# Moving the PSUM evacuations of the layernorm and the v projection from VectorE to ScalarE

## The reference

```python
x = x + attn(layernorm(x))      # x: (8, 2048, 1024), one batch element per core
x = x + ffn(layernorm(x))

def attn(x):                    # W_qkv: (16, 1024, 192), W_out: (16, 64, 1024)
    qkv = einsum('bsd,ndh->bnsh', x, W_qkv); q, k, v = split(qkv, 3)
    a = softmax(einsum('bnqh,bnkh->bnqk', q, k) / 8 + causal_mask)
    out = einsum('bnqk,bnkh->bnqh', a, v).reshape(B, -1, S)
    return einsum('bds,nhd->bsd', out, W_out)
def ffn(x):                     # w1: (1024, 4096), w2: (4096, 1024)
    return einsum('bsw,wd->bsd', relu(einsum('bsd,dw->bsw', x, w1) + b1), w2) + b2
```

## Time and profile before

| | us |
|---|---|
| median of 2 runs | 1385.1 |
| the two runs | 1368.73, 1401.48 |
| the profiled execution | 1383.07 |
| its span on the slowest core (core 2) | 1381.5 |
| spans of the eight cores | 1353.6 to 1381.5 |
| granted TensorE clock, mean of each core | 0.877 to 0.887 |

### The profile page before, as it was taken

One profiled execution on the slowest core, in us unless ns is written; L12 is line 12 of the kernel. 1 busy time (PEld: TensorE's weight loads), 2 busy tenths in 40 slices (PEclk: granted clock), 3 DMA queues, 4 the chain that ended last, 5 costly groups with the idle time before them and its releaser, 6 DMA issues.

```text
span 1381.5 us, 12666 instructions; the slowest of 8 cores (1353.6 to 1381.5 us)
## 1 busy us (share of the span) xinstructions
PE 1001.5 (72%) x4656; PEld 395.7 (29%) x4656; DVE 530.4 (38%) x686; ACT 364.9 (26%) x395; POOL 100.9 (7%) x131
## 2 busy tenths in 40 slices
PE   1155678958585858585867368898879878988897
PEld 0022332212121212131211033343324333443343
DVE  0454444363635354535443543404331323223201
ACT  0000005647475747575667300000000000000000
POOL 2100020000000000000000001020012011111110
PEclk9988998879797979797987679998989889989899
DMA  9900044100000000200020037897869779896976
GB/s 244 123 0 0 1 38 39 16 0 9 7 9 8 0 1 1 31 1 1 0 31 1 0 43 110 122 151 145 121 101 152 152 101 142 125 181 94 139 116 139
DMA packets 94331, 93.17 MB, mean 67 GB/s; under 512 B 40000, under 2 KB 72768, under 8 KB 94272
## 3 DMA queue, kind: packets, MB, share of 16 engines
q0 software_dynamic: 85248, 75.57, 39.7%
q1 hardware_dynamic: 9024, 16.80, 4.0%
HBM read 159.54 MB, written 8.39 MB: 122 GB/s over the span
## 4 chain that ended last, share of the span: by engine, by line
PE 61%; DVE 17%; DMA 13%; issue 4%; ACT 2%; DVEq 2%; POOL 0%; ACTq 0%; POOLq 0%
PE arena L718 16%; PE arena L673 12%; PE arena L506 10%; DMA wstage<-w 9%; PE arena L363 9%; PE arena L451 5%; PE arena L286 5%; DVE tmp_sb L601 4%; DVE oscr_sb L523 3%; DVE x_sb L612 3%; DMA wstage<-wout 2%; DVEq L51 2%; PE arena L466 2%; PE arena L239 1%; DVE lnf_sb L247 1%
## 5 line engine op out<-in xcount | busy, mean ns | idle before, releaser
L479 ACT ACTIVATE p_sb<-arena,cst_sb 128x1024 bf16<-128x1024 f32 (+1 forms) x320 | 291.2, 986 | 100.0 <-PE arena L451 61.7
L506 PE MATMUL arena<-p_sb,vaug_h 128*128 128x512 bf16 (+3 forms) x640 | 192.6, 387 | 146.6 <-DVE oscr_sb L523 95.3
L673 PE MATMUL arena<-lnf_sb,wstage 128*128 128x512 bf16 x1024 | 252.0, 411 | 63.4 <-DMA wstage<-w 55.8
L718 PE MATMUL arena<-w2stage,h_sb 128*128 128x512 bf16 x1024 | 221.7, 379 | 4.0 <-DVE h_sb L686 4.0
L686 DVE TENSOR_SCALAR h_sb<-arena,b1c_sb 128x512 bf16<-128x512 f32 x128 | 96.1, 751 | 217.4 <-PE arena L673 217.4
L673 PEld LDWEIGHTS arena<-lnf_sb,wstage 128*128 128x128 bf16 x1024 | 105.2, 104 | 209.2 <-issue 109.8
L718 PEld LDWEIGHTS arena<-w2stage,h_sb 128*128 128x128 bf16 x1024 | 99.9, 98 | 125.8 <-issue 5.9
L363 PE MATMUL arena<-lnf_sb,wstage 128*128 128x512 bf16 x512 | 125.1, 401 | 5.2 <-DMA wstage<-wqkv 5.2
L451 PE MATMUL arena<-qpair,kpair 64*128 64x512 bf16 (+3 forms) x640 | 124.8, 386 | 4.8 <-DVE kpair L386 4.8
L203 ACT ACTIVATE rsd_sb<-bag_sb,cst_sb 128x4 f32<-128x4 f32 x8 | 2.4, 298 | 456.3 <-DVE bag_sb L199 456.2
L239 PE MATMUL arena<-identb_sb,lntm_sb 128*128 128x128 bf16 x256 | 27.7, 279 | 109.9 <-DVE lntm_sb L223 97.9
(11 more groups left out here) (37 smaller groups left out, 452.8 us busy)
## 6 DMA issues: line engine op xcount, KB each, us to landing
wstage<-w POOLq DMA_DIRECT2D x32, 1024.0 KB, 10.7
w2stage<-w POOLq DMA_DIRECT2D x64, 512.0 KB, 7.0
x_sb<-x SPq DMA_DIRECT2D x4, 2048.0 KB, 24.9
y<-y_sb SPq DMA_DIRECT2D x16, 512.0 KB, 6.5
wstage<-wqkv POOLq DMA_DIRECT2D x24, 256.0 KB, 12.7
wstage<-wout POOLq DMA_DIRECT2D x4, 512.0 KB, 21.8
b1c_sb<-b SPq DMA_DIRECT2D x32, 0.5 KB, 7.2
identb_sb<-identf POOLq DMA_DIRECT2D x1, 32.0 KB, 8.6
```

The lines of the kernel that those rows point to most:

```text
L479: e.activation(AP(p_sb, (si_ % 3) * 1024, [[3 * 1024, 128], [512, 2], [1, w_]]), AP(arena, b_ + off_, [[AR, 128], [512, 2], [1, w_]]), AF. ...
L506: e.matmul(AP(arena, (4 + hx) * 512 + off_, [[AR, 128], [1, w_]]), vaug_h[:, hx, j_ * 128:(j_ + 1) * 128], AP(p_sb, (si_ % 3) * 1024 + hx ...
L673: (lambda s_, dc_, fb_, wp_: lambda e: e.matmul(bankap(fb_, TF), AP(wstage, s_ * 1024 + dc_ * 512 + wp_ * 128, [[8 * 1024, 128], [1, 128]] ...
L718: (lambda s_, ww_, c2_, dh_, t_: lambda e: e.matmul(bankap(t_, 512), h1_sb[:, ww_, 128 * c2_:128 * (c2_ + 1)], w2stage[:, s_, 512 * dh_:51 ...
```

## The change

The copy in `ln_transpose` and the copy in `emit_v_chunk` are issued on ACT, as an ACTIVATE with the function Identity, in place of a `tensor_copy` on DVE, and raise `ex` instead of `vv`. What waited for them waits for `ex`. The score regions at banks 2, 3 and 6, 7 and the accumulator banks of attention get waits on the last of these copies. Nothing else is changed: tiles, buffers, order of the list and all other operations are as before.

```diff
--- before.py
+++ after.py
@@ -185,7 +185,7 @@
         ln_bank_free = [("vv", 0), ("vv", 0)]
         ln_tm_free = [("tp", 0)] * 4
         ex_rstd_last = [0]
-        lnf_state = {"ready": 0}
+        lnf_state = {"ready": ("ex", 0)}
 
         def ln_stats(src_col, idx, extra_v=()):
             pb = idx % 2
@@ -244,15 +244,16 @@
                     skip_group_check=True))(pb, dc, buf),
                     waits=w0, inc="tp" if dc == DC - 1 else None)
             free_tbl[pb] = ("tp", tp_last)
-            vv_ev = add("vector", (lambda t0, p_, d_: lambda e: e.tensor_copy(
+            ex_ev = add("scalar", (lambda t0, p_, d_: lambda e: e.activation(
                 d_[:, :, t0:t0 + 128],
                 AP(arena, (2 * (p_ % 2)) * 512,
-                   [[AR, 128], [128, 8], [1, 128]])))(
+                   [[AR, 128], [128, 8], [1, 128]]),
+                AF.Identity))(
                 dst_tok0, pb, dst_sb),
-                waits=[("tp", tp_last)], inc="vv")
-            ln_bank_free[pb % 2] = ("vv", vv_ev)
-            lnf_state["ready"] = vv_ev
-            return vv_ev
+                waits=[("tp", tp_last)], inc="ex")
+            ln_bank_free[pb % 2] = ("ex", ex_ev)
+            lnf_state["ready"] = ("ex", ex_ev)
+            return ("ex", ex_ev)
 
         def ln_apply(src_col, idx, dst_sb, dst_tok0, parity, vv_rstd,
                      extra_tp=()):
@@ -267,10 +268,10 @@
                 [[64, NH], [1, HD]])
             wv_slots.append((s, dw))
         v_bank_free = [("vv", 0), ("vv", vv_wb)]
-        vv_vaug_done = 0
+        vv_vaug_done = ("ex", 0)
         last_v_mm = 0
 
-        def emit_v_chunk(c, vv_lnf_c):
+        def emit_v_chunk(c, lnf_c_rdy):
             nonlocal vv_vaug_done, last_v_mm
             pb = c % 2
             b0 = 4 + 2 * pb
@@ -280,7 +281,7 @@
                     s, dwv = wv_slots[dcc]
                     w0 = [dwv]
                     if h == 0 and dcc == 0:
-                        w0 += [("vv", vv_lnf_c), ("vv", vv_vones),
+                        w0 += [lnf_c_rdy, ("vv", vv_vones),
                                v_bank_free[pb]]
                     mm_last = add("tensor",
                                   (lambda s_, h_, dc_, c_, b_: lambda e: e.matmul(
@@ -292,12 +293,13 @@
                                   waits=w0,
                                   inc="mm" if (h == 1 and dcc == DC - 1) else None)
             last_v_mm = mm_last
-            vv_ev = add("vector", (lambda c_, b_: lambda e: e.tensor_copy(
+            ex_ev = add("scalar", (lambda c_, b_: lambda e: e.activation(
                 v_all[:, c_, 0:1024],
-                AP(arena, b_ * 512, [[AR, 128], [1, 1024]])))(c, b0),
-                waits=[("mm", mm_last)], inc="vv")
-            v_bank_free[pb] = ("vv", vv_ev)
-            vv_vaug_done = vv_ev
+                AP(arena, b_ * 512, [[AR, 128], [1, 1024]]),
+                AF.Identity))(c, b0),
+                waits=[("mm", mm_last)], inc="ex")
+            v_bank_free[pb] = ("ex", ex_ev)
+            vv_vaug_done = ("ex", ex_ev)
 
         vv_rstd_q = [0] * 4
         lnf_rdy_t = [None] * TC
@@ -323,9 +325,9 @@
             slot_free[s] = ("mm", last_v_mm)
 
         qk_bank_free = [("vv", 0), ("vv", 0)]
-        s_reg_free = [("ex", 0)] * 3
+        s_reg_free = [vv_lnf1, vv_vaug_done, ("ex", 0)]
         REG_BASE = [1024, 3072, 0]
-        o_bank_free = [("vv", vv_vaug_done), ("vv", vv_vaug_done)]
+        o_bank_free = [vv_vaug_done, vv_vaug_done]
         vv_attn_done = 0
         ex_attn_done = 0
         vaug_free = [("mm", 0), ("mm", 0)]
@@ -355,7 +357,7 @@
                         qb2 = g % 2
                         mm_last = None
                         for dcc in range(DC):
-                            w0 = ([dwqk, ("vv", vv_lnf1),
+                            w0 = ([dwqk, vv_lnf1,
                                    qk_bank_free[qb2]] + list(extra)
                                   if dcc == 0 else [])
                             mm_last = add("tensor",
@@ -408,7 +410,7 @@
                                                [128, TC], [1, 64]]),
                     AP(v_all, 64 * n_, [[TC * 1024, 128],
                                         [1024, TC], [1, 64]])))(n, hix),
-                    waits=[("vv", vv_vaug_done), ("vv", vv_vones),
+                    waits=[vv_vaug_done, ("vv", vv_vones),
                            vaug_free[hix]],
                     inc="vv")
             if npair + 1 < NH // 2:
@@ -667,7 +669,7 @@
                 fb = ww % 4
                 mm_f1 = None
                 for dcc in range(DC):
-                    w0 = ([dww, ("vv", vv_ln2), f1_bank_free[fb]]
+                    w0 = ([dww, vv_ln2, f1_bank_free[fb]]
                           if dcc == 0 else [])
                     mm_f1 = add("tensor",
                                 (lambda s_, dc_, fb_, wp_: lambda e: e.matmul(
```

## The result

The changed kernel takes 1319.5 us (median of 11 runs, 1316.1 to 1323.4) against 1384.7 us for the kernel before on the same chip: a ratio of 0.956 with a 95% interval of 0.953 to 0.959.

The account below looks back on a forecast made before the run. The bound was taken to be v-stage transposes waiting for DVE's apply, queued behind a v cast that waits for PE. From 1383.1 us, 51.9 (stage) and 6.1 (FFN starts) were subtracted: 1325 us, range 1306 to 1349.

Parts of the forecast that it names:

- Price of one copy: PSUM copy on ACT: 1.11 us, taken from the same-shape Exp row; hidden in steady chunks up to 2.0 us.
- Steady chunk: First (v) stage: PE runs back to back, so the period falls from 6.44 to 4.06 us per chunk.
- Start: Start of v stage: v(0) starts at 68.2 and ends at 73.5 us; transposes 3 and v(1) end at 77.5.
- Holes: v stage, chunks 4 and 8: PE waits 2.9 us each behind Sqrt, plus 1.4 us of lost clock each.
- Stage: First transpose to last v matmul: ends at 141.8 instead of 193.7, 51.9 us less; bounds 139.0 to 147.8.
- Attention at nothing: Attention: same instructions per engine, new waits on work already over, so priced at 0.
- FFN starts: Ahead of four FFN groups: lnf copies begin sooner on ACT, 1.6 us in group 0, 1.5 x 3 after, together 6.1.
- more idle time on w1 loads: FFN: a listed sign of being wrong, PE waiting longer for w1 weight loads; no size given.
- A: v stage stays at lower clock: chunk 6.82, stage 118, whole 1366 us, chance 0.04; beside it, 13/16 clock gives about 1340.
- B: ACT reloads tables between Sqrt and Identity, 7 x 1.28 = 9 us on the path: 1334 us; chance 0.08.
- C: Start of attention set by a DMA that doesn't move, up to 52 us lost: 1377 us, no change; chance 0.03.
- D: ACT's copies become the bound, from 2.0 us each; some 5.0 us a copy gives 1413 us; chance 0.01.

Follow-up runs that it names:

- the second profile: The changed kernel run once more with nothing altered, for a second profile: profiled execution 1315.6 us, median 1317.3 us.
- both kernels with half loads: Changed kernel, and the same with lnf copies ahead of FFN back on DVE, each with w1 loads halved in groups 1 to 3: 1288.1 and 1287.9 us.
- the first run of the reordered kernel: Kernel before with apply of chunk c+1 ahead of the v cast of c-2 on DVE, nothing on ACT: executions 1351.9 to 1435.2 us, no ratio.

## Why the prediction was right, and where its terms were off

The bound that it named, an apply behind a v cast that waits for PE, is shown: v alone on ACT and a new order on DVE give the same stage, 88.4 and 88.7 us, and lnf alone leaves it at 123.5.

- *Price of one copy*: 1.11 taken, 1.02 measured. Hidden in the steady chunks, as said: 16 more copies cost 3.7 us, nearly all of it at the two holes.
- *Steady chunk*: 4.06 predicted, 3.90 measured. The 4.06 was read from the first transpose to the end of the last v matmul, and counted the tail of that matmul, over which the next one starts. From start to start it would have been right; 48 matmuls in 10.52 already said 3.5 for a v group instead of 3.62. Over 13 chunks this is 2.1 us.
- *Start*: v(0) at 3.4 us after the first transpose, measured 3.1; v(0) itself 4.7 instead of 5.3; ahead of it PE was idle for 0.4 us, before for 2.4 us twice.
- *Holes*: 2.9 predicted, 2.82 measured, at chunks 4 and 8 and not at 12. Their price in clock, 1.4 taken between 0 and 4.4, is 1.7 and 1.5 (5.30 and 5.09 against 3.62). Taking both holes away saved 8.6 us of 2 x (2.82 + 1.6) = 8.8. The nearest hole was a fair guess and partly luck: the length alone doesn't set the price. With lnf alone on ACT a hole of 2.49 us (ahead of 97.33) was followed by transposes of 0.61 and v matmuls of 3.62, and the next, of 2.50 (ahead of 103.89), by transposes of 1.01.
- *Stage*: 77.0 predicted, 73.9 measured (74.7 on core 2); with its bounds of 74.2 to 83 the mean lies just outside, because the bounds were put on the holes alone and the error was in the steady chunk.
- *Attention at nothing*: right within its scatter; the q/k wait moved with the v matmuls.
- *FFN starts*: 6.1 us predicted as gained and kept. The starts gave more, 8.0. But "the other loads are released by FFN1 matmuls and move with them" failed: w1 waits took back about 5 of the 8. This is the step of the prediction that was wrong, and it is small only because the term was. It looked at the two loads issued ahead, which indeed had landed, and took the later ones to be fixed in length. The prediction had listed "more idle time on w1 loads" as a sign of being wrong, and that sign came.
- *Rivals*: A (the lower level throughout): out, the mean granted clock of the stage rose to 0.95. B: three table loads in all, as before, and none between a Sqrt and an Identity. C: out, the q/k matmuls moved with the last v matmul. D: out, a copy takes 1.02. A granted clock between the two levels, 0.81, came on two cores of the first profiled execution (last section). That this execution took 1339.9 us, near the 1340 named beside A, is chance: its slowest core took 12 us longer in the v stage and 15 in the attention, which the estimate did not contain.

The forecast of 1325 was thus 5.5 us high. By the means of the cores the change is 60.4 us and the sum was 58.0: the stage gave 3.2 more, attention 2.4 more than nothing, the FFN part 2.8 less (3.3 against 6.1). That the errors of stage and FFN cancel is luck. The other 3 us lie in what the sum was subtracted from, the slowest core of one execution (1383.1). That core lay 14 us behind the mean of cores at its last matmul, and the slowest of the changed kernel's profile 7, which no term of the sum could see. If the change brings the cores closer together was not tested.

## What to carry to other kernels

When two engines are each half idle and wait for each other, look at what stands in the in-order queue ahead of the instruction that the bound engine needs; moving an evacuation to an idle engine and moving it behind that instruction in its own queue cure the same steady wait, and the second needs no other engine. Count a period from start to start. And price an earlier start only after asking which stream behind it is at its limit: here a stage fed by DMA took back about 5 of 8 us, while the gain in the v stage, which was bound by engines, was kept.

## What the hardware showed beside this

In the first profiled execution of the changed kernel, cores 2 and 3 ran the steady v chunks at a granted clock that is neither of the two levels. Windows of core 1, then of core 2, for the same 11 us:

```profile
86.00:97.00 11.00, 8.83 (x53) 4.31 (x51) 1.19 (x4) 5.08 (x6) 0.00 (x0) 1.00 0.00 0
...
86.00:97.00 11.00, 11.00 (x61) 5.36 (x59) 2.68 (x6) 5.39 (x6) 0.00 (x0) 0.81 0.00 0
```

And on core 2:

```profile
90.49 0.70 PE L239 MATMUL arena<-identb_sb,lntm_sb 128*128 128x128 bf16 x8
91.01 4.37 PE L287 MATMUL arena<-wstage,lnf_sb 128*128 128x512 bf16 x16
```

Granted 0.81: a v group takes 4.37 where it takes 3.62, transposes 0.70 instead of 0.61, and the stage 85.8 and 85.5 us instead of 74, on two of the four cores of a die. The prediction had weighed the Trainium skill (TensorE: Matmul & The Clock Gate, Part 1, the peak-current limiter), which gives 13/16 = 0.81 for a die with three cores in dense matmuls, and held the trace of before against it. This execution agrees with that figure, 4.37 / 3.62 being 1.21 and 16/13 being 1.23. It does not agree on when: in the second profile all eight cores ran the same dense stage at 73.3 to 74.7 us, and cores 0 and 1 of the same die were not held here. Four more of the fourteen profiles have such stretches, from one moment on (within 1 us) always on both cores of a pair: 2 and 3 in both kernels with half loads, 4 and 5 with lnf alone on ACT, 0 and 1 together with 6 and 7 in the first run of the reordered kernel. Where they begin in the v stage or in attention (73 to 201 us), they end, broken by spells at the lower level, 157 to 203 us later. So all of them reach into the attention part, which takes 579 to 586 us on such cores and 566 to 573 on the others of these five profiles. What sets it off was not tried.
